# A graph-attention layer on one core: values in a row, projections dealt anew, paired block transposes, edge map and root on GpSimd

## Chip, core and metric

The kernel runs on one core of a Trainium2 chip. The metric is device time in microseconds (us) from the first to the last instruction and what lies around them; lower is better. The engines are called by the profile's names: PE (TensorE; PEld is its weight load), DVE (VectorE), ACT (ScalarE), POOL or Pool (GpSimd) and SP (SyncE, which issues the DMAs).

## What is computed

There are B = 32 graphs of N = 256 nodes with D = 384 features, H = 12 heads of 32. For each graph and head:

```
q = x @ Wq + bq;  k = x @ Wk + bk;  v = x @ Wv + bv        # split in 12 heads of 32
scores = q @ k.T / sqrt(32) + beta * adj
scores = where(adj > 0, scores, -9e15)
out    = softmax(scores) @ v                                # heads joined again
y      = layernorm(x + out)                                 # no scale, no shift
```

All is fp32. `adj` has an edge in one place of 128.

## The kernel before

**Data layout.** T = 2 tiles of 128 rows hold a graph's nodes, C = G = 3 tiles of 128 its features. Four heads lie in one group of 128 features (J = 4), so a graph has three groups of scores. The products with the weights are made in three passes of a high and a low part each (`xt_high`, `xt_low`, `w_high`, `w_low`), nine matmuls for one projection.

**Jobs.** All of PE's work but the scores is cut into jobs, each of which writes one of NJ = 4 PSUM banks, `j_bank`. Their kinds: X (turns 128 columns of x, L391; ACT copies the high part, then DVE subtracts it for the low part, L533 and L611), Q, K and V (projections; ACT copies them out, L529 and L531), T (turns the probabilities of a head that doesn't go by blocks; ACT copies it, L525), O (the values of four heads, probabilities times v, in packed matmuls of 32 columns, L411; ACT copies it to `heads_t`, L539), G (turns `heads_t` back, L419; DVE scales it by the inverse row sums into `att`, L618). A job `(kind, a, n)` is part `a` for graph `n`.

**What sets the order.** It is written out by hand: `jobs_of(n, h)` names for step h (0 to 11, a head) of graph n the jobs of that step. All jobs in a row form the `ring`, and job r uses bank r modulo 4. Before PE starts job r it waits until job r - 4 has been taken out of that bank by all its readers (`run`, `wait_taken`): for an X these are ACT and, after it, DVE. While graph n's heads go through softmax, PE projects graph n + 1, turns x of n + 2 and makes values and G of n - 2. The scores of a group (L458, four heads packed in rows, own banks `s_bank`) are issued by PE after the jobs of steps 0, 4 and 8: groups 1 and 2 of graph n and group 0 of graph n + 1.

**ACT** does in step h first the two exponentials of head h + 2 (`exps`, L513), then copies out the jobs of step h. **DVE** runs one head further ahead with the masked maxima (`maxima`, L595: negated scores plus bias, and their minimum), heads h + 3 and h + 4 in the steps with h mod 4 = 1, head h + 4 in those with 2 and 3. It also turns the first ten heads' probabilities in 32x32 blocks (`turn_blocks`, L630), makes the edge map of graph n + 2 (`edges`, L643: minus 9e15 where there is no edge) in step 11, and the moments for the norm. **Pool** scales the adjacency by beta and adds the edge map (`bias`, L839, L843), adds x to the values (L855), makes the root by three Newton steps on 128x2 (`layer_norm`, L868 to L878) and applies it (L881). **SP** waits for the blocks of a graph, shuffles them in 16 DMAs (`shuffle`), and loads x and adj and stores the result.

```
if r >= NJ:
    wait_taken(pe, r - NJ)          # in run(job): the bank's last job has been read
```

Of the kernel before, what the change touches and what calls it, by code (L numbers as in the profile page):

```python
# [18 lines left out]
I32 = mybir.dt.int32  # L19
ALU = mybir.AluOpType  # L20
# [14 lines left out]
def graph_attention_program(nc, x, adj, wq, bq, wk, bk, wv, bv, beta, out):  # L35
# [8 lines left out]
    NX = 5  # L44
# [4 lines left out]
    CHAIN = 4 * NEWTON + 2  # L49
# [15 lines left out]
    def jobs_of(n, h):  # L65
# [14 lines left out]
        elif n < B - 1:  # L80
            jobs = {
                0: (("O", 0, n - 2),),
                1: (("X", 0, n + 2), ("K", 0, n + 1)),
                2: (("G", 0, n - 2), ("Q", 0, n + 1)),
                3: (("K", 1, n + 1),),
                4: (("O", 1, n - 2),),
                5: (("X", 1, n + 2), ("Q", 1, n + 1)),
                6: (("G", 1, n - 2), ("Q", 2, n + 1)),
                7: (("V", 0, n + 1),),
                8: (("O", 2, n - 2),),  # L90
                9: (("X", 2, n + 2), ("K", 2, n + 1)),
                10: (("G", 2, n - 2),),
                11: (("V", 1, n + 1),),
            }
        else:
            jobs = {
                0: (("O", 0, n - 2),),
                1: (("O", 1, n - 2),),
                2: (("G", 0, n - 2), ("O", 2, n - 2)),
                3: (("G", 1, n - 2),),  # L100
                4: (("G", 2, n - 2),),
                5: (("O", 0, n),),
                7: (("G", 0, n), ("O", 0, n - 1)),
                8: (("O", 1, n - 1),),
                9: (("G", 0, n - 1), ("O", 2, n - 1)),
                10: (("G", 1, n - 1), ("O", 1, n)),
                11: (("G", 2, n - 1),),
            }
# [7 lines left out]
    last_jobs = (("O", 2, B - 1), ("G", 1, B - 1), ("G", 2, B - 1))  # L116
# [4 lines left out]
    turned_before = [0]  # L121
    for step in range(B * H):
        turned_before.append(turned_before[-1] + (not by_blocks(step // H, step % H)))


    heads_slot = {job[1:]: i % 2 for i, job in enumerate([job for job in ring if job[0] == "O"])}
# [18 lines left out]
    with ctx:  # L145
# [23 lines left out]
        v_sb = sb("v_sb", [P, 4, T, D])  # L169
# [8 lines left out]
        heads_t = sb("heads_t", [P, 2, N])  # L178
# [5 lines left out]
        nt_a = sb("nt_a", [P, T])  # L184
        nt_b = sb("nt_b", [P, T])
        nt_c = sb("nt_c", [P, T])
# [44 lines left out]
        var_ready = sem("var_ready")  # L231
# [56 lines left out]
        def wait_probs_free(eng, s):  # L288


            if s >= NX:
                before = s - NX
                if by_blocks(before // H, before % H):
                    wait(eng, blocks_ready, before + 1 - turned_before[before])
                else:
                    wait_job(eng, ("T", before % H, before // H))
# [4 lines left out]
        def _(sp):  # L301
# [11 lines left out]
            def shuffle(n):  # L313
# [3 lines left out]
                sp.wait_ge(blocks_ready, HV * n + heads)  # L317
# [47 lines left out]
        def _(pe):  # L365
# [28 lines left out]
            def values(g, n, b):  # L394
# [6 lines left out]
                for k in range(T):  # L401
                    for j in range(J):
# [8 lines left out]
                        mm = pe.matmul(b[HD * j:HD * (j + 1), 0:N], v_sb[:, n % 4, k, h * HD:(h + 1) * HD],  # L411
# [95 lines left out]
        def _(act):  # L507
# [9 lines left out]
            def take(job):  # L517
# [12 lines left out]
                elif kind == "V":  # L530
                    ins = nc.scalar.activation(v_sb[:, n % 4, a, :], b[:, 0:D], ACT.Identity)  # L531
# [50 lines left out]
        def _(dve):  # L582
# [82 lines left out]
            def moments_pair(i):  # L665
# [5 lines left out]
                else:  # L671
                    sum_with_x(n, slice(2 * P, D))
                    dve.wait_ge(part_summed, 2)
# [8 lines left out]
            def norm_last():  # L682
# [13 lines left out]
                take(("G", 1, B - 1))  # L696
# [3 lines left out]
                dve.wait_ge(part_summed, 4)  # L700
# [248 lines left out]
```

## Time and profile before

| | |
|---|---|
| median of three runs | 626.31 us (624.33, 626.31, 626.74) |
| profiled execution: own time | 624.5 us |
| its span, first to last instruction | 622.6 us |
| PE busy | 601.6 us (97%) |
| DVE busy | 591.8 us (95%) |
| ACT busy | 576.8 us (93%) |
| POOL busy | 400.9 us (64%) |
| DMA queue that carries nearly all | 81.2% of 16 engines |
| granted TensorE clock, mean | 0.989 |

The page's slices show PE, DVE and ACT busy in nine tenths or more of nearly every slice; the clock is at its upper level in all but the first slice and the last. In a timeline a row is one instruction or several of one form in a row; its first number is the start of the first, the second the time until the last has ended. Matmuls overlap, so the distance between two starts, not the busy time, is what a job takes of PE. The same goes for the other engines: an instruction begins before the one ahead of it has quite ended.

### The profile page before, as it was taken

How to read it: one execution, taken by the hardware profiler on the slowest of the kernel's cores; microseconds unless marked ns; L12 is line 12 of the kernel's file. 1: busy time of each engine (PE TensorE's matmuls, PEld its weight loads, DVE VectorE, ACT ScalarE, POOL GpSimd, SP SyncE). 2: the span in 40 equal slices, each digit the busy share in tenths (PEclk: the TensorE clock that was granted, in tenths of full speed). 3: DMA queues.
4: the chain of work that ended last, by engine and by line, in shares of the span. 5: the costliest groups of instructions: out<-in, count | busy, mean ns of one | idle time of the engine just before them, and what ended most of it. 6: DMA issues, size and time to landing. Idle time of an engine off the chain costs nothing. (4 is left out here: it accounts for less than half of the span.)

```text
span 622.6 us, 20663 instructions
## 1 busy us (share of the span) xinstructions
PE 601.6 (97%) x6080; PEld 488.0 (78%) x6080; DVE 591.8 (95%) x2266; ACT 576.8 (93%) x2063; POOL 400.9 (64%) x639
## 2 busy tenths in 40 slices
PE   7899999999999999999999999999999999999991
PEld 6887878787878888787878787888878787878850
DVE  4989999999999999999999999999999999999885
ACT  4899999999999999999999999999999999999981
POOL 1333327667767766776766776776677676677664
PEclk8999999999999999999999999999999999999996
DMA  6248889988889988889998888998888998887832
GB/s 197 83 107 193 182 170 227 188 200 203 197 201 203 223 184 205 199 202 195 222 195 196 198 202 197 205 222 183 203 203 200 196 222 189 203 202 174 192 92 103
DMA packets 68223, 117.63 MB, mean 189 GB/s; under 512 B 10512, under 2 KB 36368, under 8 KB 68112
## 3 DMA queue, kind: packets, MB, share of 16 engines
q1 hardware_dynamic: 67024, 116.10, 81.2%
q8 instruction: 51, 0.84, 0.6%
q14 instruction: 60, 0.49, 0.3%
q10 hardware_dynamic: 1088, 0.20, 0.2%
HBM read 22.94 MB, written 12.58 MB: 57 GB/s over the span
## 5 line engine op out<-in xcount | busy, mean ns | idle before, releaser
L513 ACT ACTIVATE probs<-neg_scores,neg_max 128x256 f32<-128x256 f32 x768 | 382.2, 503 | 5.0 <-DVE neg_max L595 1.4
L595 DVE CUSTOM_DVE_ANT_0 neg_scores<-s_bank,bias_sb 128x256 f32<-128x256 f32 x768 | 279.7, 415 | 9.7 <-PE s_bank L458 7.7
L630 DVE STREAM_TRANSPOSE blocks<-probs 128x512 f32<-128x512 f32 x308 | 196.7, 686 | 0.0
L513 ACT ACTIVATION_READ_ACCUMULATOR probs<-neg_scores,neg_max 128x1 f32 x768 | 149.0, 194 | 0.0
L839 POOL TENSOR_SCALAR adj_sb<-adj_sb,beta_col 128x512 f32<-128x512 f32 x31 | 62.2, 2007 | 81.4 <-DVE bias_sb L643 81.4
L458 PE MATMUL s_bank<-qk 32*128 32x256 f32 x1536 | 110.0, 400 | 2.3 <-DVE neg_max L595 1.6
L382 PE MATMUL j_bank<-xt_high,w_high 128*128 128x256 f32 x567 | 110.6, 303 | 0.4 <-DVE xt_low L611 0.3
L529 ACT ACTIVATE qk<-j_bank,qk_bias 128x256 f32<-128x256 f32 x192 | 90.0, 470 | 17.1 <-PE j_bank L382 15.3
L458 PEld LDWEIGHTS s_bank<-qk 32*128 32x128 f32 x1536 | 69.4, 184 | 42.4 <-ACT qk L529 13.2
L881 POOL TENSOR_SCALAR att<-att,rstd,shift 128x384 f32<-128x384 f32 x58 | 95.6, 1656 | 6.3 <-POOL shift L878 6.3
L411 PE MATMUL j_bank<-shuffled,v_sb 128*32 128x256 f32 x1232 | 98.1, 385 | 0.2 <-ACT blocks L525 0.2
L382 PE MATMUL j_bank<-xt_high,w_low 128*128 128x256 f32 x567 | 97.0, 279 | 0.0
L382 PE MATMUL j_bank<-xt_low,w_high 128*128 128x256 f32 x567 | 96.8, 279 | 0.0
L382 PEld LDWEIGHTS j_bank<-xt_high,w_high 128*128 128x128 f32 x567 | 79.2, 189 | 2.3 <-issue 1.3
L382 PEld LDWEIGHTS j_bank<-xt_low,w_high 128*128 128x128 f32 x567 | 79.6, 188 | 0.0
L382 PEld LDWEIGHTS j_bank<-xt_high,w_low 128*128 128x128 f32 x567 | 79.6, 188 | 0.0
L855 POOL TENSOR_TENSOR att<-att,x_sb 128x768 f32<-128x768 f32 x30 | 55.5, 1850 | 31.6 <-DVE att L618 31.6
L411 PEld LDWEIGHTS j_bank<-shuffled,v_sb 128*32 128x32 f32 x1232 | 37.2, 109 | 35.2 <-issue 15.1
L595 DVE DVE_READ_ACCUMULATOR2_ANT neg_max<- 128x1 f32 x768 | 64.5, 84 | 0.0
L849 POOL TENSOR_TENSOR x_sb<-x_sb,bv_row 128x768 f32<-128x768 f32 x32 | 59.1, 1846 | 8.2 <-DMA bv_row<-in_L_gnn_bv_dram 8.2
L611 DVE TENSOR_TENSOR xt_low<-j_bank,xt_high 128x256 fp32r<-128x256 f32 x96 | 40.1, 422 | 8.0 <-ACT xt_high L533 7.3
L379 PE MATMUL j_bank<-w_high,xt_high 128*128 128x384 f32 x192 | 46.7, 351 | 0.5 <-ACT probs_t L525 0.5
(82 smaller groups left out, 864.4 us busy)
## 6 DMA issues: line engine op xcount, KB each, us to landing
shuffled<-blocks SPq DMA_DIRECT2D x480, 160.0 KB, 4.1
x_sb<-in_x_dram SPq DMA_DIRECT2D x32, 384.0 KB, 6.0
out_dram<-att SPq DMA_DIRECT2D x30, 384.0 KB, 3.6
adj_sb<-in_adj_dram SPq DMA_DIRECT2D x32, 256.0 KB, 6.1
shuffled<-blocks SPq DMA_DIRECT2D x16, 128.0 KB, 2.7
blocks<-in_L_gnn_Wq_dram SPq DMA_DIRECT2D x1, 576.0 KB, 5.7
blocks<-in_L_gnn_Wk_dram SPq DMA_DIRECT2D x1, 576.0 KB, 8.0
blocks<-in_L_gnn_Wv_dram SPq DMA_DIRECT2D x1, 576.0 KB, 5.1
```

The source lines that it names most:

```text
L379: mm = pe.matmul(b[:, 0:D], xp[:, n % 2, c, a * P:(a + 1) * P], wp[:, q, c, :], start=(m == 0), stop=(m == 3 * C - 1))
L382: mm = pe.matmul(b[:, 0:N], wp[:, q, c, a * P:(a + 1) * P], xp[:, n % 2, c, :], start=(m == 0), stop=(m == 3 * C - 1))
L411: mm = pe.matmul(b[HD * j:HD * (j + 1), 0:N], v_sb[:, n % 4, k, h * HD:(h + 1) * HD], probs_k, start=(k == 0), stop=(k == T - 1))
L458: mm = pe.matmul(s_bank[j][:, t * N:(t + 1) * N], qk[rows, n % 2, 0, g, t * P:(t + 1) * P], qk[rows, n % 2, 1, g, :], start=True, stop=True)
L513: nc.scalar.activation(probs[:, (T * s + t) % (T * NX), :], neg_scores[:, (T * s + t) % (T * NH), :], ACT.Exp, bias=neg_max[:, n % 2, t, h ...
L529: ins = nc.scalar.activation(qk[:, n % 2, q, a, :], b[:, 0:N], ACT.Identity, bias=qk_bias[:, q, a:a + 1])
L595: nc.vector.tensor_tensor_reduce(neg_scores[:, (T * s + t) % (T * NH), :], s_bank[h % J][:, t * N:(t + 1) * N], bias_sb[:, n % 2, t, :], - ...
L630: nc.vector.transpose(blocks[:, n % 2, :, h, :, :].rearrange("p k t q -> p t k q"), probs[:, slot:slot + T, :].rearrange("p t (k q) -> p t ...
L839: nc.gpsimd.tensor_scalar(adj_sb[:, :, :], adj_sb[:, :, :], 0.0, beta_col[:, 0:1], ALU.max, ALU.mult).then_inc(adj_beta_ready, 1)
L849: nc.gpsimd.tensor_tensor(x_sb[:, n % XB, :, :], x_sb[:, n % XB, :, :], bv_row[:, :].unsqueeze(1).to_broadcast([P, T, D]), ALU.add).then_i ...
L855: nc.gpsimd.tensor_tensor(att[:, n % 3, :, :], att[:, n % 3, :, :], x_sb[:, n % XB, :, :], ALU.add).then_inc(y_ready, 1)
L881: nc.gpsimd.tensor_scalar(att[:, n % 3, t, :], att[:, n % 3, t, :], rstd[:, t:t + 1], shift[:, t:t + 1], ALU.mult, ALU.subtract).then_inc( ...
```

## The change

1. The order of jobs in graphs 1 to 30. The three O stand behind one another in steps 2, 3 and 4, ahead of the scores of group 2. Projections of Q and K move: K0 to step 0, Q0 to step 1, K1 to step 6, Q1 to step 9, K2 to step 10, Q2 to step 11; V0 to step 5, V1 stays in a step of its own, 7. Step 8 has no job left. G0, G1 and G2 stand in steps 5, 6 and 9.
2. The order in graph 31, and the jobs after it, are new as well: G of graph 29 in steps 5 to 7, the three O of graph 30 in step 8, the last two jobs are O2 and G2 of graph 31.
3. `turn_blocks` turns two heads in one instruction, in steps with h mod 4 = 0 and 3; the waits for `blocks_ready` count pairs. NX, the number of heads whose probabilities are held, is 6 instead of 5; `v_sb` has 3 places instead of 4, `heads_t` 3 instead of 2.
4. The edge map of graphs 2 to 31 is made on Pool, ahead of the scaling, after the maxima of the graph that used the same half of `bias_sb`.
5. The root on Pool: each Newton step is two instructions for each of the two columns (128x1) with operands read from columns, in place of four on 128x2.
6. `sum_with_x` of graph 30 is one DVE addition over all columns.

```
-    NX = 5
+    NX = 6
+    TURNS = ((0, 1), (2, 3), (4, 5), (6, 7), (8, 9))
+    turn_of = {h: i for i, heads in enumerate(TURNS) for h in heads}
...
-    CHAIN = 4 * NEWTON + 2
+    CHAIN = 2 * T * NEWTON + 3
...
-                8: (("O", 2, n - 2),),
-                9: (("X", 2, n + 2), ("K", 2, n + 1)),
...
+                4: (("O", 2, n - 2),),
+                5: (("X", 1, n + 2), ("G", 0, n - 2), ("V", 0, n + 1)),
...
-    heads_slot = {job[1:]: i % 2 for i, job in enumerate([job for job in ring if job[0] == "O"])}
+    heads_slot = {job[1:]: i % 3 for i, job in enumerate([job for job in ring if job[0] == "O"])}
...
-                sp.wait_ge(blocks_ready, HV * n + heads)
+                sp.wait_ge(blocks_ready, len(TURNS) * n + turn_of[heads - 1] + 1)
...
-            def turn_blocks(n, h):
-
-                dve.wait_ge(exp_ready, T * (H * n + h + 1))
-                if h == 0 and n >= 2:
+            def turn_blocks(n, heads):
+
+                first, last = heads[0], heads[-1]
+                dve.wait_ge(exp_ready, T * (H * n + last + 1))
+                if first == 0 and n >= 2:
                     dve.wait_ge(shuffled_in[n % 2], n // 2 * J * J * DMA)
-                slot = T * (H * n + h) % (T * NX)
-                nc.vector.transpose(blocks[:, n % 2, :, h, :, :].rearrange("p k t q -> p t k q"),
-                                    probs[:, slot:slot + T, :].rearrange("p t (k q) -> p t k q", q=HD)).then_inc(blocks_ready, 1)
+                slot, rows = T * (H * n + first) % (T * NX), T * len(heads)
+                nc.vector.transpose(blocks[:, n % 2, :, first:last + 1, :, :].rearrange("p k h t q -> p (h t) k q"),
+                                    probs[:, slot:slot + rows, :].rearrange("p t (k q) -> p t k q", q=HD)).then_inc(blocks_ready, 1)
...
+                    if h % J == 0 and by_blocks(n, h):
+                        turn_blocks(n, (h, h + 1))
+                    elif h % J == 3 and by_blocks(n, h):
+                        turn_blocks(n, (h - 1, h))
...
-                    if h == 11 and n + 2 < B:
-                        edges(n + 2)
...
             def bias(n):
+                if n >= 2:
+                    pool.wait_ge(adj_in, (n + 1) * DMA)
+                    pool.wait_ge(max_ready, T * H * (n - 1))
+                    take_wait()
+                    nc.gpsimd.tensor_scalar(bias_sb[:, n % 2, :, :], adj_sb[:, :, :], 0.0, MASKED,
+                                            ALU.is_le, ALU.mult).then_inc(not_edge_ready, 1)
                 pool.wait_ge(not_edge_ready, n + 1)
...
                 for _ in range(NEWTON):
-                    link(nc.gpsimd.tensor_tensor(nt_a[:, :], rstd[:, :], rstd[:, :], ALU.mult))
-                    link(nc.gpsimd.tensor_tensor(nt_b[:, :], nt_a[:, :], var_eps[:, :], ALU.mult))
-                    link(nc.gpsimd.tensor_scalar(nt_c[:, :], nt_b[:, :], -0.5, 1.5, ALU.mult, ALU.add))
-                    link(nc.gpsimd.tensor_tensor(rstd[:, :], rstd[:, :], nt_c[:, :], ALU.mult))
+                    for t in range(T):
+                        linked(rstd_at[t])
+                        b_at[t] = link(nc.gpsimd.tensor_scalar(nt_b[:, t:t + 1], var_eps[:, t:t + 1], rstd[:, t:t + 1],
+                                                               rstd[:, t:t + 1], ALU.mult, ALU.mult))
+                    for t in range(T):
+                        linked(b_at[t])
+                        rstd_at[t] = link(nc.gpsimd.tensor_scalar(rstd[:, t:t + 1], nt_b[:, t:t + 1], 1.5, rstd[:, t:t + 1],
+                                                                  ALU.add, ALU.mult))
```

What the new order puts around the X of step 9 on PE. Before, from that X to the job that needs its bank again (`xt_high,w_high` is a projection's first pass, `ident,probs` a T, `ident,heads_t` a G, `128x384` a V):

```order
L391 MATMUL j_bank3<-ident,x_sb 128x128 x2
L382 MATMUL j_bank0<-xt_high,w_high 128x256 x3
L382 MATMUL j_bank0<-xt_low,w_high 128x256 x3
L382 MATMUL j_bank0<-xt_high,w_low 128x256 x3
L428 MATMUL j_bank1<-ident,probs 128x128 x4
L419 MATMUL j_bank2<-ident,heads_t 128x128 x2
L428 MATMUL j_bank3<-ident,probs 128x128 x4
L379 MATMUL j_bank0<-w_high,xt_high 128x384 x3
```

After, from the same X on:

```order
L383 MATMUL j_bank1<-ident,x_sb 128x128 x2
L411 MATMUL j_bank2<-ident,heads_t 128x128 x2
L374 MATMUL j_bank3<-xt_high,w_high 128x256 x3
L374 MATMUL j_bank3<-xt_low,w_high 128x256 x3
L374 MATMUL j_bank3<-xt_high,w_low 128x256 x3
L420 MATMUL j_bank0<-ident,probs 128x128 x4
L374 MATMUL j_bank1<-xt_high,w_high 128x256 x3
```

The X of step 9 wrote bank 3 and a T took it next; now it writes bank 1, a G, a K or Q and a T follow, and the next projection (K2, step 10) takes bank 1.

The same for the X of step 5 on PE. Before:

```order
L391 MATMUL j_bank1<-ident,x_sb 128x128 x2
L382 MATMUL j_bank2<-xt_high,w_high 128x256 x3
L382 MATMUL j_bank2<-xt_low,w_high 128x256 x3
L382 MATMUL j_bank2<-xt_high,w_low 128x256 x3
L419 MATMUL j_bank3<-ident,heads_t 128x128 x2
L382 MATMUL j_bank0<-xt_high,w_high 128x256 x3
L382 MATMUL j_bank0<-xt_low,w_high 128x256 x3
L382 MATMUL j_bank0<-xt_high,w_low 128x256 x3
L379 MATMUL j_bank1<-w_high,xt_high 128x384 x3
```

After:

```order
L383 MATMUL j_bank3<-ident,x_sb 128x128 x2
L411 MATMUL j_bank0<-ident,heads_t 128x128 x2
L371 MATMUL j_bank1<-w_high,xt_high 128x384 x3
L371 MATMUL j_bank1<-w_high,xt_low 128x384 x3
L371 MATMUL j_bank1<-w_low,xt_high 128x384 x3
L411 MATMUL j_bank2<-ident,heads_t 128x128 x2
L374 MATMUL j_bank3<-xt_high,w_high 128x256 x3
```

Before, two projections and a G stood between and a V took the bank (1); now G0, V0 and G1 stand between, and K1 of step 6 takes bank 3.

On ACT, from the copy of Q2 in step 6 to the copy of K2 in step 9, before (a `probs` row with x2 is the two exponentials of one head):

```order
L529 ACTIVATE qk<-j_bank0,qk_bias 128x256
L513 ACTIVATE probs,row_sum<-neg_scores,neg_max 128x256 x2
L531 ACTIVATE v_sb<-j_bank1 128x384
L513 ACTIVATE probs,row_sum<-neg_scores,neg_max 128x256 x2
L539 ACTIVATE heads_t<-j_bank2 128x4x2x32
L513 ACTIVATE probs,row_sum<-neg_scores,neg_max 128x256 x2
L533 ACTIVATE xt_high<-j_bank3 128x256
L529 ACTIVATE qk<-j_bank0,qk_bias 128x256
```

After, from the copy of K1 in step 6 to that of Q1 in step 9:

```order
L521 ACTIVATE qk<-j_bank3,qk_bias 128x256
L505 ACTIVATE probs,row_sum<-neg_scores,neg_max 128x256 x2
L523 ACTIVATE v_sb<-j_bank0 128x384
L505 ACTIVATE probs,row_sum<-neg_scores,neg_max 128x256 x4
L525 ACTIVATE xt_high<-j_bank1 128x256
L521 ACTIVATE qk<-j_bank3,qk_bias 128x256
```

Between the copy of a V in step 7 and that of the third X lay two exponentials, the copy of an O and two exponentials; now there are four exponentials.

On ACT after the change, from the copy of Q0 in step 1 to that of V0 in step 5:

```order
L521 ACTIVATE qk<-j_bank3,qk_bias 128x256
L505 ACTIVATE probs,row_sum<-neg_scores,neg_max 128x256 x2
L531 ACTIVATE heads_t<-j_bank0 128x4x2x32
L505 ACTIVATE probs,row_sum<-neg_scores,neg_max 128x256 x2
L531 ACTIVATE heads_t<-j_bank1 128x4x2x32
L505 ACTIVATE probs,row_sum<-neg_scores,neg_max 128x256 x2
L531 ACTIVATE heads_t<-j_bank2 128x4x2x32
L505 ACTIVATE probs,row_sum<-neg_scores,neg_max 128x256 x2
L525 ACTIVATE xt_high<-j_bank3 128x256
L523 ACTIVATE v_sb<-j_bank1 128x384
```

The three copies of O and eight exponentials lie between the copy of Q0 and that of the second X.

## Rows read from the trace of the kernel before

**Rows 1.** Stretches: length; PE, PEld, DVE, ACT, POOL busy; PEclk, DMA share, GB/s.
```profile
300.00:400.00 100.00, 99.89 (x1029) 80.57 (x1020) 98.75 (x376) 96.15 (x348) 71.28 (x120) 1.00 0.90 202
...
600.00:623.00 23.00, 8.37 (x100) 4.49 (x90) 15.08 (x52) 7.80 (x23) 10.79 (x34) 0.76 0.23 83
```

**Rows 2.** DVE timeline, two edge maps: start, us, engine, line, operation.
```profile
93.09 0.39 DVE L643 TENSOR_SCALAR bias_sb<-adj_sb 128x512 f32<-128x512 f32 x1
...
552.72 0.40 DVE L643 TENSOR_SCALAR bias_sb<-adj_sb 128x512 f32<-128x512 f32 x1
```

**Rows 3.** PE's timeline in one graph of the middle.
```profile
298.18 0.55 PE L382 MATMUL j_bank<-xt_high,w_high 128*128 128x256 f32 x3
...
299.37 1.07 PE L411 MATMUL j_bank<-shuffled,v_sb 128*32 128x256 f32 x16
...
302.75 0.38 PE L419 MATMUL j_bank<-ident,heads_t 128*128 128x128 f32 x2
302.88 0.60 PE L382 MATMUL j_bank<-xt_high,w_high 128*128 128x256 f32 x3
...
304.03 0.69 PE L379 MATMUL j_bank<-w_high,xt_high 128*128 128x384 f32 x3
...
305.69 0.41 PE L411 MATMUL j_bank<-shuffled,v_sb 128*32 128x256 f32 x2
...
305.93 0.39 PE L411 MATMUL j_bank<-shuffled,v_sb 128*32 128x256 f32 x2
...
306.14 0.39 PE L411 MATMUL j_bank<-shuffled,v_sb 128*32 128x256 f32 x2
...
306.69 1.15 PE L458 MATMUL s_bank<-qk 32*128 32x256 f32 x16
307.76 0.44 PE L391 MATMUL j_bank<-ident,x_sb 128*128 128x128 f32 x2
307.96 0.60 PE L382 MATMUL j_bank<-xt_high,w_high 128*128 128x256 f32 x3
...
309.11 0.60 PE L428 MATMUL j_bank<-ident,probs 128*128 128x128 f32 x4
309.54 0.38 PE L419 MATMUL j_bank<-ident,heads_t 128*128 128x128 f32 x2
309.76 0.60 PE L428 MATMUL j_bank<-ident,probs 128*128 128x128 f32 x4
310.12 0.77 PE L379 MATMUL j_bank<-w_high,xt_high 128*128 128x384 f32 x3
```

**Rows 4.** ACT timeline, same stretch; in brackets the wait before and its releaser.
```profile
305.79 0.49 ACT L531 ACTIVATE v_sb<-j_bank 128x384 f32<-128x384 f32 x1
306.19 0.51 ACT L513 ACTIVATE probs<-neg_scores,neg_max 128x256 f32<-128x256 f32 x1
...
307.19 0.36 ACT L539 ACTIVATE heads_t<-j_bank 128x256 f32<-128x256 f32 x1
307.46 0.50 ACT L513 ACTIVATE probs<-neg_scores,neg_max 128x256 f32<-128x256 f32 x1
...
308.44 0.36 ACT L533 ACTIVATE xt_high<-j_bank 128x256 fp32r<-128x256 f32 x1
309.31 0.47 ACT L529 ACTIVATE qk<-j_bank,qk_bias 128x256 f32<-128x256 f32 x1 [0.50 <-PE j_bank L382]
```

**Rows 5.** DVE's timeline, the low part of a turned x, same stretch.
```profile
308.83 0.42 DVE L611 TENSOR_TENSOR xt_low<-j_bank,xt_high 128x256 fp32r<-128x256 f32 x1
```

**Rows 6.** Start-up: DVE's low parts, and the PE projection that waited for them.
```profile
18.77 1.09 DVE L611 TENSOR_TENSOR xt_low<-j_bank,xt_high 128x256 fp32r<-128x256 f32 x3 [0.36 <-ACT xt_high L533]
...
20.00 0.60 PE L382 MATMUL j_bank<-xt_high,w_high 128*128 128x256 f32 x3 [0.30 <-DVE xt_low L611]
```

**Rows 7.** The page's part 5, Pool's scaling of the adjacency.
```profile
L839 POOL TENSOR_SCALAR adj_sb<-adj_sb,beta_col 128x512 f32<-128x512 f32 x31 | 62.2, 2007 | 81.4 <-DVE bias_sb L643 81.4
```

**Rows 8.** Pool's timeline, one link of the root's chain.
```profile
300.39 0.20 POOL L875 TENSOR_TENSOR nt_b<-nt_a,var_eps 128x2 f32<-128x2 f32 x1 [0.18 <-POOL nt_a L874]
```

More of the change, by code:

```diff
@@ L115, in graph_attention_program @@
     second_jobs = (("K", 1, 0),) + tuple(("X", c, 1) for c in range(C))
-    last_jobs = (("O", 2, B - 1), ("G", 1, B - 1), ("G", 2, B - 1))
+    last_jobs = (("O", 2, B - 1), ("G", 2, B - 1))
     ring = [*first_jobs, *second_jobs, *(job for n in range(B) for h in range(H) for job in jobs_of(n, h)), *last_jobs]
     place = {job: r for r, job in enumerate(ring)}
-    turned_before = [0]
-    for step in range(B * H):
-        turned_before.append(turned_before[-1] + (not by_blocks(step // H, step % H)))
-    heads_slot = {job[1:]: i % 2 for i, job in enumerate([job for job in ring if job[0] == "O"])}
+    heads_slot = {job[1:]: i % 3 for i, job in enumerate([job for job in ring if job[0] == "O"])}
     def on_act(job):
@@ L168, in graph_attention_program @@
         qk = sb("qk", [P, 2, 2, G, N])
-        v_sb = sb("v_sb", [P, 4, T, D])
+        v_sb = sb("v_sb", [P, 3, T, D])
         neg_scores = sb("neg_scores", [P, T * NH, N])
@@ L177, in graph_attention_program @@
         shuffled = sb("shuffled", [P, 2, T, J, HV, T, HD])
-        heads_t = sb("heads_t", [P, 2, N])
+        heads_t = sb("heads_t", [P, 3, N])
         att = sb("att", [P, 3, T, D])
@@ L293, in wait_probs_free @@
                 if by_blocks(before // H, before % H):
-                    wait(eng, blocks_ready, before + 1 - turned_before[before])
+                    wait(eng, blocks_ready, len(TURNS) * (before // H) + turn_of[before % H] + 1)
                 else:
@@ L410, in values @@
                                 probs_k = probs_k.rearrange("p (t a q) -> p a t q", t=T, a=J)
-                        mm = pe.matmul(b[HD * j:HD * (j + 1), 0:N], v_sb[:, n % 4, k, h * HD:(h + 1) * HD],
+                        mm = pe.matmul(b[HD * j:HD * (j + 1), 0:N], v_sb[:, n % 3, k, h * HD:(h + 1) * HD],
                                        probs_k, start=(k == 0), stop=(k == T - 1))
@@ L530, in take @@
                 elif kind == "V":
-                    ins = nc.scalar.activation(v_sb[:, n % 4, a, :], b[:, 0:D], ACT.Identity)
+                    ins = nc.scalar.activation(v_sb[:, n % 3, a, :], b[:, 0:D], ACT.Identity)
                 elif kind == "X":
@@ L790, in _ @@
                         maxima(s + 4)
-                    if h % J == 0:
-                        turned_now = (h,)
-                    elif h % J == 3 and h < HV:
-                        turned_now = (h - 2, h - 1, h)
-                    else:
-                        turned_now = range(2 * J + 1, HV) if h == 2 * J + 2 else ()
-                    for head in turned_now:
-                        if by_blocks(n, head):
-                            turn_blocks(n, head)
+                    if h % J == 3:
+                        for job in jobs_of(n, h):
+                            if job[0] == "G":
+                                take(job)
+                    if h % J == 0 and by_blocks(n, h):
+                        turn_blocks(n, (h, h + 1))
+                    elif h % J == 3 and by_blocks(n, h):
+                        turn_blocks(n, (h - 1, h))
                     if h == 0 and n >= 1:
@@ L806, in _ @@
                         moments(n - 3)
[L807 to L808 removed]
                     if h % J != 1:
                         for job in jobs_of(n, h):
[L811 removed]
+                            if job[0] not in ("", "", "TG", "G")[h % J]:
                                 take(job)
@@ L857, in layer_norm @@
             def layer_norm(n):
-                step = [0]
+                step = [CHAIN * n]
                 def link(ins):
@@ L862, in link, with linked @@
                     ins.then_inc(chain, 1)
-                    pool.wait_ge(chain, CHAIN * n + step[0])
+                    return step[0]
+                def linked(count):
+                    pool.wait_ge(chain, count)
                     take_wait()
```

66 lines of the change are left out of this document (29 added, 37 removed).

## Prediction

> **What bounds the kernel now.** I read the page's busy shares first, then the busy time by stretch, then each engine's own timeline through one graph of the middle. In the 100 us from 300 on [rows 1] PE is busy for 99.89, DVE for 98.75, ACT for 96.15 and Pool for 71.28, at the upper clock (2.4 GHz, PEclk 1.00). Two engines are as good as full, so no busy share tells which one sets the pace. The edge map is made once a graph: its starts at 93.09 and 552.72 [rows 2] lie 25 graphs apart, so a graph takes 459.63 / 25 = 18.39 us. In PE's timeline [rows 3] job follows job at fixed distances, with no hole that a wait would leave. PE's order and its switches between kinds of matmul make up the whole period; DVE, with some 0.2 us to spare in 18.4, is a close second, and ACT has about 0.7. So two questions decide: what does PE's new order sum to, and does every other engine still hand back PE's banks in time?
>
> **PE's new order, summed.** I take distances between starts of jobs, each with the switch to the next [rows 3]: projection to packed values 1.19 (298.18 to 299.37); G to projection 0.13 (302.75 to 302.88); projection to the next unpacked job 1.15 (302.88 to 304.03, and 307.96 to 309.11); V to packed 1.66 (304.03 to 305.69); values to scores 1.00 (305.69 to 306.69); scores to X 1.07; X to projection 0.20; T to projection or V 0.36 (309.76 to 310.12); G to T 0.22. Three distances aren't in the trace. Values behind values: four rounds of four matmuls at 0.21 to 0.24 (305.69, 305.93, 306.14), so 0.88; bounds 0.84, and 1.00 if it cost what values to scores cost. X to G: G to T is 0.22 and X to projection is 0.07 above G to projection, so 0.28; bounds 0.20 and 0.43 (T to G, 309.11 to 309.54). V to G: 1.66 like V to packed; bounds 1.50 and 1.75. Then one graph is, in order:
> steps 0 and 1, K0 1.19, scores 1.07, X 0.20, Q0 1.19: 3.65;
> steps 2 to 4, O 0.88, O 0.88, O 1.00: 2.76;
> steps 4 to 7, scores 1.07, X 0.28, G 0.13, V0 1.66, G 0.13, K1 1.15, V1 1.66: 6.08;
> steps 8 to 11, scores 1.07, X 0.28, G 0.13, Q1 1.15, T 0.36, K2 1.15, T 0.36, Q2 1.15: 5.65.
> Sum 18.14 against 18.39: **the order alone gives 0.25 us a graph** (0.05 to 0.35 between the bounds). It comes from two switches between packed values and their neighbours that are gone.
>
> **The bank of the third X.** The rule of the four banks bites here. The X of step 9 is followed by G2, Q1 and T, and the fourth job behind it, K2, needs its bank. K2 may start when ACT has copied the high part and DVE has made the low one. PE gets from the start of V1 to the start of K2 in 1.66 + 1.07 + 0.28 + 0.13 + 1.15 + 0.36 = 4.65 us. ACT can't run ahead of V1: it copies a V 1.76 after PE has begun it (304.03, and 305.79 in [rows 4]), goes on after 0.40 (to 306.19), then has four exponentials, 0.98 to 1.00 for two (307.46 to 308.44, 306.19 to 307.19), 1.98 in all, and begins the X 4.14 after V1 began. Its copy takes 0.36; DVE begins 0.03 later (308.44 + 0.36 = 308.80, then 308.83 in [rows 5]) and takes 0.42; PE begins 0.14 after DVE's end (18.77 + 1.09 = 19.86, then 20.00, [rows 6]). Together 5.09. **PE waits 5.09 - 4.65 = 0.44 us a graph** (bounds 0.25 and 0.6, from the bounds above and 0.05 for each of ACT's steps). The same sum for the kernel before shows no wait, as its rows do: one O more lay between, 1.00 of PE but 0.27 of ACT (307.19 to 307.46), and the X of 307.76 was four jobs away from the T of 309.76, when DVE had been done since 308.83 + 0.42 = 309.25.
>
> **The bank of the second X.** The X of step 5 is followed by G0, V0 and G1, and K1 takes its bank. ACT is held by Q0: it copies a projection 1.35 after its start (307.96, and 309.31 with a wait of 0.50 [rows 3, 4]). Then come 0.37 for that copy (a V's 0.40, a little less), four pairs of exponentials at 0.985, 3.94, and three O at 0.27, 0.81, all ahead of the X: 6.47, and with 0.36, 0.03, 0.42 and 0.14 7.42. PE comes from Q0 to K1 in 1.19 + 2.76 + 1.07 + 0.28 + 0.13 + 1.66 + 0.13 = 7.22. **The wait is 0.20** (bounds 0 and 0.35): four pairs of exponentials and five copies of ACT stand against a stretch in which PE runs through three values in 2.76. DVE reaches that X about then, too: it can begin the eighth head's maxima only when the scores are there. The two waits don't share time, since ACT's chain begins anew at Q0 and at V1. What is queued behind the PE that waits are K2, then T, Q2, K0 and scores, and K1, V1 and scores; everybody behind them is shifted alike, so nothing is won back.
>
> **What leaves DVE.** The edge map, 0.39 a graph [rows 2], and the fixed share of five of ten block transposes; no row has a transpose of 1024 elements a partition, so I bound that share at 0 and 0.1 each. DVE falls from 18.2 (98.75% of 18.39 [rows 1]) to 17.3 to 17.8. This is worth nothing while PE and ACT's chain end last. Of the maxima's place around the blocks: in front of each first maximum of a group there are still over 2 us of blocks, under which PE's scores (1.07 and their tail) hide. At zero I also put NX = 6 and the third place of `heads_t`: they only permit. If DVE had set the pace, they and the edge map would be the gain; the fourth place of `v_sb` isn't missed, since V0 comes after O2.
>
> **What Pool gets.** The edge map there is priced by the scaling of the adjacency, same size: 2.01 us [rows 7], plus one wait for its own result of 0.18 [rows 8]. Bounds 1.3 and 2.3. The root had 15 links of 0.19 and 0.18, 5.7 in all; now it has nine waits on its path and 15 small instructions, 3.4 at best and, if operands read from a column make each one dearer by 0.1, up to 6. Pool was busy 13.1 of 18.39 [rows 1] and waited for itself some 3.2; now it is 16.2 + 2.2 and between - 2.3 and + 0.3 more, 16.1 to 18.7. That stays under the new period of 18.8, and both results have a graph's time until they are asked for. SP's store stands behind the bias in its queue and moves by some 2 us, against a shuffle whose values are read more than a graph later.
>
> The Trainium skill (GPSIMD Engine Reference, section Performance versus the Vector engine) speaks against this part: elementwise work stays on DVE, where it finds GpSimd about 2 times slower. The rows are worse than that, 2.01 against 0.39. By the page's ratio the edge map would cost Pool 0.8, and Pool would end near 16 in place of 17 to 18. Neither changes the end.
>
> **Start and end.** Graph 0 keeps its order. Graphs 2 to 29, 28 of them, have the full pattern. Graph 1 has no values and graph 30 no X; each may gain some 0.3. From 600 us on PE is busy for only 8.37 of 23 us [rows 1]; the end hangs on Pool's last norms and on DVE. PE has some switches fewer there and DVE fewer instructions, but G of graph 29, on which Pool's last norms wait, comes three steps later: 0, within -1.5 and +1.5.
>
> **The sum.** Per graph -0.25 + 0.44 + 0.20 = +0.39 us; 28 times, 10.9; less 0.6, 10.3. On the profiled execution's 624.5 us (span 622.6) that is 634.8, period 18.8. The median of before, 626.31, lies 1.8 above that execution, which is one of the faster; half to all of it comes on top, so 636.0.
>
> **Rivals.** *Faster than before*: the banks are free in time. ACT's chain is the one place: if it reached the third X 0.44 and the second 0.20 earlier (because an exponential pair costs less when DVE and Pool are lighter, or PE's V1 to K2 takes longer than I sum), the 0.25 of the order remain, 28 times 0.25 is 7 and the ends 0.6, and 617 on the profiled execution or 619 as a median results. It decides where the two waits together fall below 0.25. For it: the sum of the first wait hangs on a distance that I estimated (X to G). Against it: four exponentials cannot shrink, 1.98 of 5.09 is theirs, and a PE wait of this very kind is in rows 6. Chance 0.14. *The waits eat the gain and no more*: together 0.14 to 0.36, 623 to 628. Chance 0.11. *Only the third X's bank is late*: +0.19 a graph, 5.3 less 0.6, 630.5. Chance 0.15. *Pool becomes the bound*: with column operands dearer than I allow, above 18.8; at 19.2, 28 times 0.8 is 22 and the result 648. Chance 0.05. *DVE was the bound, PE merely kept step*: then PE's sum would show holes behind DVE, and there are none; it is contained in the faster case. The forecast has 0.55.
>
> **How the numbers follow.** Slower by over 0.5% (about what a measurement of this kernel can tell from no change) has 0.55 + 0.15 + 0.05 = 0.75, faster 0.14, within it 0.11. The range leaves out the faster case and the slow Pool: from 626, under the single wait, to 642, where both waits are at their upper bounds with the order's gain at 0.25 (0.6 + 0.35 - 0.25 = 0.7, 28 times 20, taken in part since both ends at once are unlikely).
>
> **What would show it.** In the profile of the changed kernel: PE waiting once a graph at a projection of high parts for DVE's `xt_low`, 0.4, and once more, 0.2; ACT's idle time a graph above 1 us, before copies of Q and K; DVE below 96%; values behind values at 0.88; scores 18.8 us apart from graph to graph. Wrong would be it if PE stood at 100% with a period of 18.15, or if a Pool wait stood in front of the maxima.

## The result, and the profile after

The changed kernel takes 634.45 us (median of 4 runs, 633.69 to 635.19), the kernel before 625.54 beside it (624.33 to 626.74): 1.0142 times, 95% interval 1.0116 to 1.0169. Slower, as forecast (636.0, range 626 to 642). Its profiled execution took 633.69 with a span of 631.8, where 634.8 was predicted; 9.2 above the 624.5 of before.

Busy time by stretch (length; PE, PEld, DVE, ACT, Pool; clock, DMA share, GB/s), to be held against [rows 1]:

```profile
300.00:400.00 100.00, 99.17 (x1038) 80.86 (x1037) 94.67 (x342) 95.78 (x347) 86.90 (x122) 1.00 0.89 200
```

DVE is lighter by 4 points, Pool heavier by 16, and PE's share fell a little although it is PE that sets the pace. Its timeline through one graph of the middle shows where the share went (the rows answer to [rows 3]; only the first pass of a projection is kept):

```profile
302.65 2.14 PE L403 MATMUL j_bank<-shuffled,v_sb 128*32 128x256 f32 x34
...
305.38 1.15 PE L450 MATMUL s_bank<-qk 32*128 32x256 f32 x16
306.45 0.44 PE L383 MATMUL j_bank<-ident,x_sb 128*128 128x128 f32 x2
306.73 0.38 PE L411 MATMUL j_bank<-ident,heads_t 128*128 128x128 f32 x2
306.87 0.77 PE L371 MATMUL j_bank<-w_high,xt_high 128*128 128x384 f32 x3
...
308.51 0.38 PE L411 MATMUL j_bank<-ident,heads_t 128*128 128x128 f32 x2
308.79 0.59 PE L374 MATMUL j_bank<-xt_high,w_high 128*128 128x256 f32 x3
...
309.92 0.69 PE L371 MATMUL j_bank<-w_high,xt_high 128*128 128x384 f32 x3
...
312.68 0.44 PE L383 MATMUL j_bank<-ident,x_sb 128*128 128x128 f32 x2
312.96 0.38 PE L411 MATMUL j_bank<-ident,heads_t 128*128 128x128 f32 x2
313.10 0.60 PE L374 MATMUL j_bank<-xt_high,w_high 128*128 128x256 f32 x3
...
314.24 0.60 PE L420 MATMUL j_bank<-ident,probs 128*128 128x128 f32 x4
314.99 0.60 PE L374 MATMUL j_bank<-xt_high,w_high 128*128 128x256 f32 x3
...
318.78 1.15 PE L450 MATMUL s_bank<-qk 32*128 32x256 f32 x16
```

From T (314.24) to K2 (314.99) are 0.75 us, where a T stands 0.36 from the next projection in [rows 3]: the wait for the third X's bank. From G1 (308.51) to K1 (308.79) are 0.28 instead of 0.13: the wait for the second. Both are short holes without a bracket; distances show them, busy time hardly. Over all graphs they make 0.39 and 0.15 us a graph.

ACT ahead of K2 (to be held against [rows 4]; its reads of the accumulator are left out), then DVE:

```profile
311.71 0.49 ACT L523 ACTIVATE v_sb<-j_bank 128x384 f32<-128x384 f32 x1
312.10 0.50 ACT L505 ACTIVATE probs<-neg_scores,neg_max 128x256 f32<-128x256 f32 x1
...
313.57 0.50 ACT L505 ACTIVATE probs<-neg_scores,neg_max 128x256 f32<-128x256 f32 x1
...
314.07 0.37 ACT L525 ACTIVATE xt_high<-j_bank 128x256 fp32r<-128x256 f32 x1
```

```profile
307.92 0.42 DVE L587 CUSTOM_DVE_ANT_0 neg_scores<-s_bank,bias_sb 128x256 f32<-128x256 f32 x1
...
308.27 0.42 DVE L603 TENSOR_TENSOR xt_low<-j_bank,xt_high 128x256 fp32r<-128x256 f32 x1
...
314.47 0.42 DVE L603 TENSOR_TENSOR xt_low<-j_bank,xt_high 128x256 fp32r<-128x256 f32 x1 [0.74 <-ACT xt_high L525]
```

V1's copy, four exponentials, the copy of the X, DVE's low part (314.47 to 314.89), and 0.10 later K2: the chain of the prediction link by link. DVE idles 0.74 us in front of it. At 308.27 it doesn't idle: there the low part stands right behind the maxima, and ACT's copy had ended at about the same moment (307.86 and 0.38, 308.24). That will matter below.

**Where the 9.2 us are.** I take the start of a graph's group 1 of scores, the one behind step 0, in graph 2 and graph 29 of both traces: 55.72 and 552.07 before, 58.25 and 560.58 after. That is 18.383 and 18.605 us a graph, so the middle costs 27 times 0.222, 6.0 us; the start costs 2.5 and the end (70.6 and 71.2 from there to the end of the span) 0.6.

**The start.** PE at the hand-over from graph 0 to graph 1, and the DVE row it waited for:

```profile
37.56 0.79 PE L371 MATMUL j_bank<-w_high,xt_high 128*128 128x384 f32 x3 [0.47 <-ACT probs_t L517]
...
38.72 0.68 PE L371 MATMUL j_bank<-w_low,xt_high 128*128 128x384 f32 x3
40.12 0.59 PE L374 MATMUL j_bank<-xt_high,w_high 128*128 128x256 f32 x3 [0.72 <-DVE xt_low L603]
...
41.35 1.15 PE L450 MATMUL s_bank<-qk 32*128 32x256 f32 x16
```

```profile
39.55 0.43 DVE L603 TENSOR_TENSOR xt_low<-j_bank,xt_high 128x256 fp32r<-128x256 f32 x1 [0.63 <-ACT xt_high L525]
```

In graph 1's step 0 stands K0 of graph 2. It needs all three parts of x of graph 2, and the last was turned only in step 11 of graph 0. PE waits for it in front of K0, and the scores behind it start at 41.35. In the kernel before they start at 39.02 (its PE timeline at the same place):

```profile
39.02 1.15 PE L458 MATMUL s_bank<-qk 32*128 32x256 f32 x16
```

**The end.** Pool's last norms, and the DVE addition that runs beside them:

```profile
609.37 1.84 POOL L850 TENSOR_TENSOR att<-att,x_sb 128x768 f32<-128x768 f32 x1 [4.87 <-DVE att L610]
...
616.18 4.34 POOL L886 TENSOR_SCALAR att<-att,rstd,shift 128x384 f32<-128x384 f32 x2 [0.22 <-POOL shift L883]
```

```profile
615.92 0.94 DVE L656 TENSOR_TENSOR att<-att,x_sb 128x768 f32<-128x768 f32 x1
...
618.37 0.71 DVE L656 TENSOR_TENSOR shuffled<-shuffled,x_sb 128x512 f32<-128x512 f32 x1
```

Pool waits 4.87 us for G2 of graph 29, and its two norms take 4.34 in place of twice 1.65. Both come back in experiment 11, and the norms in the last section.

### The profile page after: what moved, and what is told of

Its sections match the earlier page's. It is cut to its first block and busy times, and to the rows that moved or that the text cites. A ratio compares the mean times of both kernels' runs of the same rounds, so it can differ in the third digit from the quotient of the medians.

```text
span 631.8 us, 20536 instructions
## 1 busy us (share of the span) xinstructions
PE 602.8 (95%) x6080; PEld 497.7 (79%) x6080; DVE 573.9 (91%) x2081; ACT 580.2 (92%) x2063; POOL 488.9 (77%) x669
## 5 line engine op out<-in xcount | busy, mean ns | idle before, releaser
L623 DVE STREAM_TRANSPOSE blocks<-probs 128x1024 f32<-128x1024 f32 x154 | 184.3, 1227 | 2.1 <-ACT probs L505 2.1
L403 PE MATMUL j_bank<-shuffled,v_sb 128*32 128x256 f32 x1232 | 85.9, 382 | 0.5 <-ACT blocks L517 0.5
L831 POOL TENSOR_SCALAR bias_sb<-adj_sb 128x512 f32<-128x512 f32 x30 | 58.0, 1934 | 18.5 <-DVE neg_max L587 16.0
L403 PEld LDWEIGHTS j_bank<-shuffled,v_sb 128*32 128x32 f32 x1232 | 42.9, 109 | 31.0 <-ACT blocks L517 0.7
```

The lines of the kernel that those rows point to most:

```text
L403: mm = pe.matmul(b[HD * j:HD * (j + 1), 0:N], v_sb[:, n % 3, k, h * HD:(h + 1) * HD], probs_k, start=(k == 0), stop=(k == T - 1))
L623: nc.vector.transpose(blocks[:, n % 2, :, first:last + 1, :, :].rearrange("p k h t q -> p (h t) k q"), probs[:, slot:slot + rows, :].rearr ...
L831: nc.gpsimd.tensor_scalar(bias_sb[:, n % 2, :, :], adj_sb[:, :, :], 0.0, MASKED, ALU.is_le, ALU.mult).then_inc(not_edge_ready, 1)
```

## The experiments

**The theory.** Two banks come back late, that of step 9's X by 0.39 and that of step 5's by 0.15 us a graph; without these waits the change is worth about 0.3 a graph. The start is one missed dependency. **Rivals:** the waits are an effect and not the cause (another engine, Pool or DVE, is as late, and takes their place when they go); it is Pool's new load that costs; the second X is late because of DVE's queue and not ACT's. All times below are medians; the ratio to the kernel before has its 95% interval in brackets. "Period" is the distance of the scores of group 1 from graph 2 to graph 29, over 27.

**1. The third X's bank.** ACT copies the X of step 9 ahead of the step's exponentials.

```diff
+                    early = [job for job in jobs_of(n, h) if job[0] == "X" and h in (9,)]
+                    for job in early:
+                        take(job)
                     if s + 2 < B * H:
                         exps(s + 2)
                     for job in jobs_of(n, h):
-                        take(job)
+                        if job not in early:
+                            take(job)
```

> The changed kernel, but ACT copies the X of step 9 before that step's exponentials instead of behind them. Theory of the bank wait: the wait of 0.39 us in front of K2 goes, 28 graphs, 10.9 us, so 623.5 us against 634.45 of the changed kernel. Rival one (the waits are only where another engine's lateness shows, DVE or Pool setting the pace): the time stays within 2 us of 634. Rival two (ACT's own work is next at once, since it then has to wait for the X): half the gain, 629.

Measured: 625.37 (1.0004 [0.9991, 1.0017]), 9 us less than the changed kernel; period 18.279. In its PE timeline K2 stands 0.36 behind T:

```profile
311.36 0.60 PE L420 MATMUL j_bank<-ident,probs 128*128 128x128 f32 x4
311.72 0.60 PE L374 MATMUL j_bank<-xt_high,w_high 128*128 128x256 f32 x3
```

The wait is gone in all graphs, and 0.33 of its 0.39 us came back; the 9 us are less than the 10.9 expected. The rest went to the other wait, in front of K1, that grew from 0.15 to 0.20. So the wait was the cause, for the size that its gap had. It also settles whose it was. The table of waits of the changed kernel, in the stretch from 100 to 550 us (engine, line waited for: us in total, times, longest), names a wrong releaser:

```profile
DVE xt_low L603 <- ACT xt_high L525: 17.4, 24, 0.7
...
ACT v_sb L523 <- PE j_bank L371: 11.8, 24, 0.5
PEld j_bank L374 <- ACT qk L521: 8.6, 24, 0.4
...
ACT qk L521 <- PE j_bank L374: 2.2, 12, 0.2
```

PE's 0.36 us 24 times are put down to ACT's copy of Q1, which ended at about the same time as DVE's low part. In this experiment that copy runs from 311.56 to 312.03, and K2 starts in the middle of it, at 311.72: it isn't needed. The bank that K2 takes is the X's, and DVE reads it last.

**2. The second X's bank.** The same for step 5 alone (`h in (5,)`).

> The changed kernel, but ACT copies the X of step 5 before that step's exponentials. Bank theory: the wait of 0.15 us in front of K1 goes, 28 graphs, 4.2 us, so 630.2 us. Rival (DVE reaches that X late anyhow, behind the eighth and ninth head's maxima): half or less, 632.5 to 634.5.

Measured: 633.18 (1.0129 [1.0114, 1.0144]), period 18.571, the wait at K1 0.12 instead of 0.15. The rival was right: with ACT's copy made early DVE is next, at once.

**3. Both copies early** (`h in (5, 9)`).

> The changed kernel with both X copied early. If the two waits add up, as two chains that begin anew at Q0 and V1: 0.54 us a graph, 15 us, 619.3 us, a period of 18.07 us. If ACT or Pool (17.4 us of work a graph) ends last once they are gone: 622 to 625.

Measured: 624.43 (0.9990 [0.9981, 0.9999]), period 18.263. That is what the third X alone brought. PE still waits 0.19 at K1, and DVE's timeline shows behind what:

```profile
304.20 0.39 DVE L591 CUSTOM_DVE_ANT_0 neg_scores<-s_bank,bias_sb 128x256 f32<-128x256 f32 x1
...
305.21 0.42 DVE L591 CUSTOM_DVE_ANT_0 neg_scores<-s_bank,bias_sb 128x256 f32<-128x256 f32 x1
...
305.56 0.42 DVE L607 TENSOR_TENSOR xt_low<-j_bank,xt_high 128x256 fp32r<-128x256 f32 x1
```

```profile
305.76 0.38 PE L411 MATMUL j_bank<-ident,heads_t 128*128 128x128 f32 x2
306.08 0.58 PE L374 MATMUL j_bank<-xt_high,w_high 128*128 128x256 f32 x3
```

ACT's copy of that X is done (it ended at 304.55), but DVE first makes the maxima of two heads, four instructions of 0.34 each from 304.20 on, and its low part ends at 305.98. K1 starts 0.10 later.

**4. The start.** K0 of graph 2 behind the scores, in graph 1 only.

```diff
-                0: (("K", 0, n + 1),),
-                1: (("X", 0, n + 2), ("Q", 0, n + 1)),
+                0: (("K", 0, n + 1),) if n > 1 else (),
+                1: (("X", 0, n + 2), ("Q", 0, n + 1)) if n > 1 else (("X", 0, n + 2), ("K", 0, n + 1), ("Q", 0, n + 1)),
```

> The changed kernel, but in graph 1 alone K0 stands in step 1 behind the scores and the X, as in the kernel before, not in step 0 ahead of the scores. Theory: 2.3 us of the difference arose there, since that K0 waits for the x of graph 2, turned just before in step 11 of graph 0, and holds the scores of group 1 back: 632.1 us. Rival (the start's loss is caught up later or hides under other waits): 634.5 us.

Measured: 632.42 (1.0118 [1.0101, 1.0135]), 2.0 less than the changed kernel, period 18.609. The two intervals overlap; the traces settle it. The scores of group 1 start in graph 1 at 39.17 instead of 41.35, in graph 2 at 56.50 instead of 58.25. All five traces with K0 in front have the former between 41.1 and 41.6 (the changed kernel, 1, 2, 3 and 6), and 4, 5, 8, 9 and 10, with K0 behind, between 39.0 and 39.5. So this K0 cost some 2 us at the start and nothing of the middle.

**5. Experiments 3 and 4 together.**

> The changed kernel with both X copied early and K0 of graph 1 behind the scores: 634.45 - 15.1 - 2.3 = 617.0 us by the bank theory, below the 625.5 of the kernel before by 8.5. If the order's own saving of 0.3 us a graph was not real, it ends at 625.

Measured: 623.09 (0.9970 [0.9958, 0.9981]), period 18.266: 6 us above the 617.0 of the bank theory, as experiment 3 was 5 above its 619.3. The start's gain comes on top of experiment 3's, 1.3 us, and the wait at K1, still there behind DVE's maxima, keeps the time above 617.

**6. The edge map back on DVE**, in step 11 of the changed kernel.

```diff
+                    if h == 11 and n + 2 < B:
+                        edges(n + 2)
```

> The changed kernel with the edge map made by DVE in step 11 as before; the rest of the change stays. Bank theory: DVE waits 0.74 us a graph for ACT's copy of the third X, so 0.39 us more of work costs nothing: 634.5 us, within 1. Rival, DVE sets the pace: 28 times 0.3 is 9 us more, 643.

Measured: 634.34 (1.0144 [1.0130, 1.0159]), period 18.591. Busy in the 100 us from 300 on:

```profile
300.00:400.00 100.00, 99.25 (x1035) 81.56 (x1034) 95.99 (x352) 96.04 (x347) 75.86 (x113) 1.00 0.89 200
```

Pool is lighter by 11 points and DVE heavier by 1.3, at the same time. Where the edge map stands is worth nothing here.

**7. Only the Pool parts of the change, on the kernel before**: edge map and new root, with the old order and single turns.

> The kernel before with two parts of the change alone: edge map on Pool and the new root on Pool; order, single blocks and buffers as before. If PE's order sets the pace of the kernel before: 625.5 us, within 1. If DVE did (98.8% busy), it gains up to 0.39 us a graph, 30 times, 11: 614. If Pool slows its neighbours: above 627.

Measured: 623.56 (0.9979 [0.9971, 0.9988]), period 18.349 against 18.383. Pool is at 88.61 in the stretch of [rows 1] and PE at 100.00. A gain of 0.2%, 0.9 below the band that was expected; the Pool parts are excluded as the cause of the loss. They take 0.03 us a graph off the old order, and PE's share rises from 99.89 to 100.00: the kernel before had small holes where the prediction saw none. Which of the two parts closes them isn't separated.

**8. The edge map back on DVE in experiment 5's kernel.**

> The kernel with both X early and the start mended, and the edge map back on DVE. At a period of 18.07 us DVE would have 17.3 to 17.5 us of work plus 0.39: if that still hides, 617 us; if DVE's late second X then holds K1 again, 0.2 to 0.4 us a graph, 623 to 628.

Measured: 624.24 (0.9988 [0.9980, 0.9997]), period 18.287. That is 1.1 us above experiment 5, but the two intervals touch, and the periods differ by 0.02, 0.6 us in all. So the edge map off DVE is worth little even there, where DVE's low part is what K1 waits for (the wait is 0.21 instead of 0.19).

**9. DVE's half of the second wait.** On top of experiment 5, DVE makes step 5's low part and G between the two heads' maxima, as it already does in step 9.

```diff
-                        if h != 2 * J + 1 and s + 4 < B * H:
+                        if h not in (5, 9) and s + 4 < B * H:
...
-                        if h == 2 * J + 1 and s + 4 < B * H:
+                        if h in (5, 9) and s + 4 < B * H:
```

> The kernel with both X early and the start mended, and on DVE in step 5 the low part of the X and the take of G0 stand between the maxima of the two heads, as they do in step 9. Theory: what still held K1, 0.19 us a graph, is DVE's queue (two heads of maxima, 1.37 us, ahead of the low part, which ends 0.10 before K1 begins); it goes: 28 times 0.19 is 5.3, 617.8 us, period 18.07. Rival: PE's wait has another source (ACT's copy, Pool), 623.1 us unchanged.

Measured: 617.24 (0.9874 [0.9857, 0.9891]), period 18.062. Neither wait is left, and PE is full (the stretch from 300 to 400, then K1 0.13 behind G1 in PE's timeline, then the DVE rows in step 5):

```profile
300.00:400.00 100.00, 100.00 (x1031) 84.90 (x1033) 97.12 (x356) 97.82 (x354) 89.62 (x116) 1.00 0.88 205
```

```profile
317.69 0.38 PE L411 MATMUL j_bank<-ident,heads_t 128*128 128x128 f32 x2
317.82 0.59 PE L374 MATMUL j_bank<-xt_high,w_high 128*128 128x256 f32 x3
```

```profile
316.45 0.42 DVE L591 CUSTOM_DVE_ANT_0 neg_scores<-s_bank,bias_sb 128x256 f32<-128x256 f32 x1
...
316.79 0.42 DVE L607 TENSOR_TENSOR xt_low<-j_bank,xt_high 128x256 fp32r<-128x256 f32 x1
```

The low part now stands behind two maxima, not four, and ends 0.6 us ahead of K1. This settles the account of the middle: 18.605 - 18.062 = 0.543 us a graph for the two waits, whose gaps in the changed kernel sum to 0.39 + 0.15 = 0.54. Without its waits the change is worth 18.383 - 18.062 = 0.32 us a graph. The Pool parts bring 0.03 of it in the old order too (experiment 7, 18.349), so 0.29 are left for the new order with its buffers and paired turns, which no run separates.

**10. The edge map back on DVE in experiment 9's kernel.**

> The kernel of the first run of this call with the edge map back on DVE in step 11. If at a period of 18.07 us DVE (17.0 to 17.3 us of work) can carry 0.39 more: 618 us, within 1. If DVE's place in the queue then holds the scores or a bank: 2 to 8 us more.

Measured: 617.99 (0.9883 [0.9868, 0.9897]), period 18.062, DVE at 98.79 in the stretch, PE at 100.00. The intervals of 9 and 10 overlap, and the periods are equal: even at 98.8% busy DVE doesn't set the pace.

**11. The end.** Experiment 9's kernel with G1 and G2 of graph 29 one step earlier.

```diff
-                5: (("G", 0, n - 2),),
-                6: (("G", 1, n - 2), ("O", 0, n)),
-                7: (("G", 2, n - 2), ("G", 0, n)),
+                5: (("G", 0, n - 2), ("G", 1, n - 2)),
+                6: (("G", 2, n - 2), ("O", 0, n)),
+                7: (("G", 0, n),),
```

> The same, and in graph 31 the G of graph 29 stand in steps 5 and 6 instead of 5 to 7. Pool waited 4.87 us for the last of them before its last norms, which end the kernel. Theory: up to 0.6 us off, until DVE's own end is last, 617.2 us. Rival: the end is set by DVE alone, 0.

Measured: 615.40 (0.9843 [0.9829, 0.9858]), the fastest of all and 1.6% below the kernel before. The gain of 1.8 over experiment 9 was expected at 0.6; the two intervals just touch. In the traces the stretch from the scores of graph 29 to the end of the span shrinks from 70.8 to 69.3, so 1.5 are the end's (the last section says why the profiled execution as a whole is the longer one, 617.52 against 616.69). Pool's timeline at the end:

```profile
593.46 1.83 POOL L854 TENSOR_TENSOR att<-att,x_sb 128x768 f32<-128x768 f32 x1 [3.48 <-DVE att L614]
...
600.26 1.65 POOL L890 TENSOR_SCALAR att<-att,rstd,shift 128x384 f32<-128x384 f32 x1 [0.22 <-POOL shift L887]
```

The wait for G2 is 3.48 instead of 4.86 in experiment 9, that is 1.4, and the norms take 3.28 instead of 4.34.

## Why the prediction was right, and where it was not

**What bounds the kernel.** Right: PE's order sets the pace, and neither DVE at 98.8% busy nor Pool at 89% does (experiments 6, 7, 10). *DVE was the bound* and *Pool becomes the bound* fell with them. Only "no hole" in the kernel before was a little too much: experiment 7 finds 0.03 us a graph there.

**PE's new order: right, the term under-sized.** 18.14 predicted, 18.06 measured with all waits gone (experiment 9), so a gain of 0.32, 0.03 of it not the order's, where I wrote 0.25; inside its bounds. The estimated distances held: three values and the switch to the scores took 2.73 (302.65 to 305.38) where 2.76 stood, X to G 0.28 (306.45 to 306.73), V0 to G1 1.64 (306.87 to 308.51) for 1.66. Two distances were taken over from a neighbour and shouldn't have been: a projection to the scores costs 1.15 (317.63 to 318.78, K0), not the 1.19 of a projection to packed values, and a projection to a V 1.13 (308.79 to 309.92; 1.11 in experiment 9), not 1.15.

**The bank of the third X: right.** 0.44 predicted, 0.39 measured, all of it given back when the copy moves. ACT began the X's copy 4.15 behind V1 (309.92, 314.07), as summed (4.14). The step that was off is the last link: from DVE's end to PE's start 0.10 (314.89, 314.99), not the 0.14 of [rows 6].

**The bank of the second X: right in size, wrong in cause.** 0.20 predicted, 0.15 measured. But the sum ran through ACT alone, and only half a sentence said that DVE reaches that X about then too. DVE's four maxima ended together with ACT's copy, so two chains of nearly equal length stood in front of K1, and moving ACT's half brought 0.03 (experiment 2). The missing step was to sum DVE's row, from the scores of step 0 on, as ACT's was summed:

```profile
301.48 0.43 DVE L587 CUSTOM_DVE_ANT_0 neg_scores<-s_bank,bias_sb 128x256 f32<-128x256 f32 x1 [0.19 <-PE s_bank L450]
```

PE began these scores at 300.14. DVE waited for them until 301.48 and ran without a gap from there to the end of the low part at 308.69: 1.34, 7.21 and 0.10 are 8.65. By the prediction's own distances PE comes from these scores to K1 in 1.07 + 0.20 + 1.19 + 2.76 + 1.07 + 0.28 + 0.13 + 1.66 + 0.13 = 8.49, so DVE's chain alone makes a wait of 0.16. In experiment 1 the two still ended together (ACT's copy at 305.40, DVE's low part from 305.43 on) with a wait of 0.20; in experiment 3, with ACT's half moved, DVE's alone left 0.19.

**The two together:** 0.39 predicted for the net of a graph, 0.22 measured: 0.07 from the order, 0.05 from each wait. Over the graphs 10.9 in the sum, 6.0 in the traces.

**DVE, Pool.** DVE fell to 94.67% of 18.605, 17.6 us a graph (17.3 to 17.8 predicted), worth nothing, as said. The edge map took 1.93 us on Pool (2.01 predicted) and the root 4.8 from its first instruction to the norm that waits for it (between 3.4 and 6). Operands read from a column made an instruction dearer by 0.14 with two of them and 0.07 with one:

```profile
305.02 0.66 POOL L876 TENSOR_SCALAR nt_b<-var_eps,rstd 128x1 f32<-128x1 f32 x2 [0.21 <-POOL rstd L869]
305.66 0.51 POOL L880 TENSOR_SCALAR rstd<-nt_b,rstd 128x1 f32<-128x1 f32 x2
```

Two take 0.66 and 0.51, 0.33 and 0.26 each, where one with constants takes 0.19 ([rows 8] has 0.20 for one on two columns).

**The start: wrong.** The text had "graph 1 may gain some 0.3"; this K0 lost about 2 (experiment 4; the pair of traces has 2.5 up to graph 2). Experiment 4's trace is still 0.8 behind the kernel before at graph 2, and why stays open. The failed step is the assumption that graph 1 is a graph of the new pattern with something left out. It is also the first in which the new pattern meets a graph 0 in the old order: K0 moved from behind the scores to in front of them, and what it reads, the last X of graph 2, was made by the old order's last step. I had followed banks through the new order, but not the data through the seam.

**The end: within its bounds of 1.5, at +0.6.** The later G of graph 29 does cost: Pool's wait for it, 4.87 in the changed kernel, and its norms that fell beside DVE's additions. Experiment 11 got some 1.5 to 1.8 back by moving them one step.

**So the sum** of 10.3 was 9.2, because the middle was 5 too dear, and the start, with graphs 1 and 30, 3 too cheap (the end 0.6). The forecast's mechanism is shown; that its number fits to 0.3% is in part these two errors cancelling.

**What the profile was to show.** The waits at K2 and K1, DVE below 96% and the values at 0.88 apart (0.87) came. Scores stood 18.6 apart, not 18.8. ACT's idle time wasn't above 1 us nor in front of Q and K: the table above has 11.8 + 2.2 us over 24 graphs, 0.58 each, most of it before copies of V. ACT had taken its X late and its Q straight after it; it was behind there, not waiting.

**The faster rival, 617,** had its condition right, since "ACT reaches the X earlier" is experiment 1's edit, and its price too: experiment 9 is at 617.24. The waits and the start are what separates the change from it.

## What to carry to other kernels

When jobs are dealt anew over a few rotating buffers, sum for each buffer the time of the engine that wants it back, and beside it the queue of *each* engine that must release it; where two such chains end together, moving one of them gains next to nothing (0.03 of 0.15 here). A short wait that repeats shows in the distance between starts, not in busy shares, and its releaser in the profile may be the neighbour that ended at the same time. And where a new order begins behind an old one, follow the data of its first round through the seam: one dependency there cost as much as a third of the loss in all the graphs behind it.

## What the runs showed of the hardware

A Pool instruction that began while DVE added two operands from SBUF did its work only when that addition was over; one that was already running wasn't slowed. In the changed kernel the first norm begins at 616.18, inside the addition of 615.92 to 616.86, and takes 2.20 in place of 1.65:

```profile
616.18 2.20 POOL L886 TENSOR_SCALAR att<-att,rstd,shift 128x384 f32<-128x384 f32 x1 [0.22 <-POOL shift L883]
```

The second begins at the same moment as the addition at 618.37 and takes 2.15; the pair takes 4.34. In experiment 11 a norm has been running since 600.26 when the addition begins (DVE's timeline), and takes its 1.65; the small instruction that begins at 603.67, under the next addition (603.50 to 604.19), takes 0.58 in place of 0.20:

```profile
601.04 0.95 DVE L660 TENSOR_TENSOR att<-att,x_sb 128x768 f32<-128x768 f32 x1
```

```profile
603.67 0.58 POOL L907 TENSOR_SCALAR pair_var<-pair_mean_var 128x4 f32<-128x4 f32 x1
```

The Trainium skill (SBUF — State Buffer, section Who interferes with whom) says that a DVE instruction with two SBUF inputs contends with a GpSimd instruction that reads SBUF, that the port pair they share is an exclusive lock, and that the order of issue decides who blocks. The first case agrees: Pool was second and was held up for 0.55. In the second Pool was first, and DVE's addition wasn't held up: 0.95, as against 0.94 where it was first. No run here shows why. How much of experiment 11's gain is this contention's isn't separated from the shorter wait by a run of its own. What the pair of traces shows is that DVE's last norm waits 0.62 for Pool in experiment 9 and not at all in experiment 11.

Executions of one kernel also differ at the start, in when PE's granted clock is lower. In experiment 3's trace PE had stood idle for 2.1 us in front of the scores at 46.16, and from 47.20 to 50.60 the clock was at 1.2 GHz (0.51 in the first row); in the changed kernel's trace PE stood idle at the same place for 2.1 us too, and the clock stayed at 2.4 GHz (second row):

```profile
47.20:50.60 3.40, 3.40 (x15) 3.36 (x12) 3.40 (x15) 1.69 (x7) 0.00 (x0) 0.51 0.93 238
```

```profile
46.40:49.80 3.40, 3.40 (x35) 3.07 (x28) 3.40 (x12) 2.89 (x11) 0.00 (x0) 1.00 1.05 250
```

The next scores start 7.22 behind these in the first and 5.67 in the second, so the lower clock cost 1.5 us. The traces of experiments 1 and 6 have it at this place as well, that of experiment 2 hasn't. Of experiment 3's ten runs eight lie between 623.80 and 624.76 and two, the profiled one among them, at 625.80 and 625.91. In experiment 11's trace the clock is at 0.50 from 13.80 to 20.60, twice as long as in experiment 9's (7.90 to 11.30), and the scores of graph 0's group 2 start 2.4 later; so its profiled execution is the longer one although its end is shorter. A difference of 1.5 us between two single executions says nothing here; periods and the stretch behind the scores of graph 29 do.
